# Moving the second half's normalisation behind the first ropes, and the second ropes' sums to Pool, in the prologue of an attention and routed-MLP kernel

## The reference

```
xn  = layernorm(x)
q, k = rope(xn @ Wq.T), rope(xn @ Wk.T); v = xn @ Wv.T      # 16 heads of 16
attn = softmax(mask(q k^T / 4)) v @ Wo.T
xm  = three-tap mix of xn along the tokens
ffn = layernorm(xn + (the one of 9 two-layer paths that the router picks for the token), gamma, beta)
out = x + attn + ffn
```

## Time and profile before

| | us |
|---|---|
| three runs | 888.17, 888.21, 890.82 |
| median | 888.21 |
| profiled execution, device time | 890.88 |
| span of the profiled execution | 889.1 |
| PE busy | 808.8 (91%) |
| VectorE busy | 627.8 (71%) |
| ScalarE busy | 478.3 (54%) |
| Pool busy | 289.7 (33%) |
| mean granted clock of PE (1.0 is full speed) | 0.964 |

### The profile page before, as it was taken

The page is one execution under the profiler, slowest core; times in us unless marked ns, Lnnn a source line. Parts: engine busy times, 40 slices in busy tenths (PEclk is TensorE's granted clock), DMA queues, the critical chain, the costliest instruction groups (busy, mean ns, idle before and its releaser), DMA issues.

```text
span 889.1 us, 13041 instructions
## 1 busy us (share of the span) xinstructions
PE 808.8 (91%) x4968; PEld 396.1 (45%) x4968; DVE 627.8 (71%) x1222; ACT 478.3 (54%) x820; POOL 289.7 (33%) x420
## 2 busy tenths in 40 slices
PE   4767999989999999989999999989999999999986
PEld 2422334344455534344355544435355554354434
DVE  5967786757678697658759688666868777767521
ACT  2452545645545655655646655655646555555572
POOL 1001023860515121781513302495140502030523
PEclk9876999989999999989999999999999999999999
DMA  6372312124222413022350623021450330300103
GB/s 214 107 177 45 75 28 45 36 72 107 51 46 46 97 49 72 1 72 76 67 96 1 119 72 64 10 72 37 108 95 2 72 73 17 56 1 1 25 1 72
DMA packets 35386, 55.15 MB, mean 62 GB/s; under 512 B 4330, under 2 KB 31667, under 8 KB 32444
## 3 DMA queue, kind: packets, MB, share of 16 engines
q1 hardware_dynamic: 30812, 49.54, 24.0%
q0 software_dynamic: 4224, 4.19, 3.2%
q10 hardware_dynamic: 288, 0.59, 0.2%
HBM read 37.27 MB, written 16.78 MB: 61 GB/s over the span
## 4 chain that ended last, share of the span: by engine, by line
PE 72%; DVE 15%; POOL 8%; ACT 2%; issue 2%; DMA 1%; SPq 1%; DVEq 0%; ACTq 0%; POOLq 0%
PE bank L1210 13%; PE bank L1171 12%; PE bank L1191 12%; PE bank L1157 8%; PE bank L1147 6%; DVE piecemax L991 5%; PE bank L1238 3%; PE bank L1168 3%; PE bank L1102 3%; PE bank L1113 2%; PE bank L1220 2%; PE bank L1120 2%; POOL prob L653 2%; POOL turned L635 2%; POOL raw L636 2%
## 5 line engine op out<-in xcount | busy, mean ns | idle before, releaser
L991 DVE TENSOR_REDUCE piecemax<-bank 128x1 f32<-128x512 f32 (+3 forms) x608 | 381.8, 656 | 181.4 <-PE bank L1171 179.6
L774 ACT ACTIVATE prob<-bank 128x512 f32<-128x512 f32 x576 | 334.4, 597 | 315.7 <-PE bank L1191 313.9
L653 POOL TENSOR_SCALAR_AFFINE_SELECT prob<-prob 128x256 f32<-128x256 f32 (+1 forms) x320 | 134.0, 433 | 429.2 <-ACT prob L774 428.0
L1171 PE MATMUL bank<-k_st,q_st 96*128 96x128 bf16 (+3 forms) x1152 | 231.4, 281 | 11.6 <-DVE piecemax L991 11.4
L1191 PE MATMUL bank<-q_st,k_st 98*128 98x512 bf16 (+3 forms) x768 | 223.3, 332 | 12.5 <-DMA q_st<-shiftT 6.4
L1210 PE MATMUL bank<-prob,v_sb 128*17 128x512 f32 (+3 forms) x1536 | 159.8, 505 | 13.3 <-POOL prob L653 13.1
L1171 PEld LDWEIGHTS bank<-k_st,q_st 96*128 96x128 bf16 x1152 | 98.6, 99 | 146.9 <-issue 63.6
L1191 PEld LDWEIGHTS bank<-q_st,k_st 98*128 98x128 bf16 x768 | 71.5, 99 | 120.7 <-ACT prob L774 51.5
L1157 PE MATMUL bank<-w_sb,mid 128*128 128x256 f32 (+1 forms) x320 | 86.7, 394 | 3.2 <-DVE z L984 3.2
L1102 PE MATMUL bank<-xnT,wqk_sb 128*128 128x512 f32 x128 | 68.3, 635 | 5.6 <-ACT xnT L709 4.7
L1147 PE MATMUL bank<-xm,w_sb 128*128 128x512 f32 x128 | 67.6, 609 | 0.0
(11 more groups left out here) (86 smaller groups left out, 721.3 us busy)
## 6 DMA issues: line engine op xcount, KB each, us to landing
scratch<-parts SPq DMA_DIRECT2D x16, 768.0 KB, 3.8
q_st<-scratch SPq DMA_DIRECT2D x90, 128.0 KB, 6.8
k_st<-scratch SPq DMA_DIRECT2D x15, 384.0 KB, 4.7
z<-in_x SPq DMA_DIRECT2D x8, 512.0 KB, 4.8
z<-in_x POOLq DMA_DIRECT2D x8, 512.0 KB, 6.0
out<-z SPq DMA_DIRECT2D x8, 512.0 KB, 3.3
k_st<-scratch SPq DMA_DIRECT2D x15, 256.0 KB, 5.4
k_st<-scratch SPq DMA_DIRECT2D x17, 128.0 KB, 5.7
```

Source lines behind the costliest of these rows:

```text
L653: nc.gpsimd.affine_select(out=d, in_=d, compare_op=ALU.is_ge, fill=0.0, base=0, pattern=pattern, channel_multiplier=-1).then_inc(masked, 1)
L774: nc.scalar.activation(prob[:, place_of(G, i), :], ps[:, :], ACT.Exp, scale=float(DK) ** -0.5).then_inc(act_took, 1)
L991: nc.vector.tensor_reduce(piecemax[:, G % 2, t, h:h + len(cols), piece], ps[:, 0:len(cols) * w].rearrange("p (h k) -> p h k", k=w), AX.X, ...
L1171: ins = nc.tensor.matmul(ps[:, k * w:(k + 1) * w], q_st[0:PARTS, G % STACKS, h, t * P:(t + 1) * P], k_st[0:PARTS, G % STACKS, h, k0:k0 + w ...
```

## The change

Two things change, both for batch 0 only.

1. In the prologue's list stats, pow and norm of the second half no longer stand ahead of the first projections. They stand behind the first half's four projections, two ropes and two hi cuts, and directly ahead of the transposes of the second half.
2. The two sums of the second half's ropes (q and k) are formed by Pool (L637, L638) and no longer by VectorE (L906, L907). VectorE still forms the products out of PSUM. Pool waits for VectorE's second unit of the rope. The predicate `sums_on_dve(n, half)` takes the place of `rope_on_dve(n)` where the semaphore and its count are chosen.

```diff
-    head("load", 0, 0)
-    head("load", 0, 1)
-    for half in range(2):
+    def normalized(half):
         head("stats", 0, 0, half)
         head("pow", 0, 0, half)
         head("norm", 0, half)
-        if half == 0:
-            turn(0)
+
+    head("load", 0, 0)
+    head("load", 0, 1)
+    normalized(0)
+    turn(0)
     project(0, 0)
     cut(0, 0, "hi")
     project(1, 0)
     cut(1, 0, "hi")
+    normalized(1)
     turn(1)
     cut(0, 0, "rest", "mid_cut")
     cut(1, 0, "rest", "mid_cut")
...
+def sums_on_dve(n, half):
+    return n == 0 and half == 0
...
-    mine = [x for x in ORDER if x[0] == "rope" and rope_on_dve(x[1]) == rope_on_dve(n)]
+    mine = [x for x in ORDER if x[0] == "rope" and sums_on_dve(x[1], x[3]) == sums_on_dve(n, half)]
...
-            return (roped_dve if rope_on_dve(n) else roped_pool), nth_rope(n, qk, half)
+            return (roped_dve if sums_on_dve(n, half) else roped_pool), nth_rope(n, qk, half)
...
-                pool.wait_ge(tables_loaded, 32)
-                pool.wait_ge(act_took, TOOK["qk", n, qk, 1, half])
-                if k >= 2:
-                    pool.wait_ge(lo_cut, NTH["lo", *from_turn(k - 2)])
-                nc.gpsimd.tensor_tensor(a, r, half_of(cos_sb, half)[:, None, :].to_broadcast(shape), ALU.mult)
-                link(nc.gpsimd.tensor_tensor(r, r, half_of(sin_sb, half)[:, None, :].to_broadcast(shape), ALU.mult))
+                if rope_on_dve(n):
+                    pool.wait_ge(dve_took, TOOK["qk", n, qk, 1, half])
+                else:
+                    pool.wait_ge(tables_loaded, 32)
+                    pool.wait_ge(act_took, TOOK["qk", n, qk, 1, half])
+                    if k >= 2:
+                        pool.wait_ge(lo_cut, NTH["lo", *from_turn(k - 2)])
+                    nc.gpsimd.tensor_tensor(a, r, half_of(cos_sb, half)[:, None, :].to_broadcast(shape), ALU.mult)
+                    link(nc.gpsimd.tensor_tensor(r, r, half_of(sin_sb, half)[:, None, :].to_broadcast(shape),
+                                                 ALU.mult))
                 nc.gpsimd.tensor_tensor(a[:, 0, :], a[:, 0, :], r[:, 1, :], ALU.subtract)
                 nc.gpsimd.tensor_tensor(a[:, 1, :], a[:, 1, :], r[:, 0, :], ALU.add).then_inc(roped_pool, 1)
...
                 elif what == "rope":
-                    if not rope_on_dve(name[1]):
+                    if not sums_on_dve(name[1], name[3]):
                         rope(*name[1:])
...
-                elif what == "rope" and rope_on_dve(name[1]):
+                elif what == "rope" and sums_on_dve(name[1], name[3]):
                     rope(*name[1:])
```

## The result

| | before | changed |
|---|---|---|
| first comparison, median of 5 | 890.74 us (888.17 to 891.87) | 896.80 us (895.27 to 900.03) |
| ratio, 95% interval | | 1.0078 (1.0048 to 1.0107) |
| second comparison, ratio | | 1.0094 (1.0081 to 1.0107) |
| span of the profiled execution | 889.1 us | 898.0 us |

The change makes the kernel slower by a little under 1%: by 7 us in the first comparison and by 8 in a second one on another set of runs. The ratios are of the means of the runs, so they need not agree with the quotient of the medians (6.1 us apart here). 7.0 was forecast, 895.2 us and a range of 892.0 to 899.3; the median 896.80 lies in it.

What follows compares the result with a forecast made beforehand. The prologue's VectorE chain was taken to set when the body begins. With the last cut at 52.0 against 45.04, 7.0 us pass on whole: median 888.21 becomes 895.2 us, range 892.0 to 899.3.

Steps and rivals of the forecast that it cites:

- What bounds: Prologue: VectorE's chain to the last cut sets when the body begins; a microsecond there is one on the end.
- Rivals 3: Body: a different phase of engines or clock gives back 4 to 7 us; 888 to 890.8; chance 0.06.
- 4 (the clock turns it round): PE's clock in 56 to 60 and 72 to 88: up to 7.6 us back, 885.0, faster; chance 0.03.
- rival 2: Maxima or next stretch: PE's longer rests leave its clock low, 2.65 us on top, up to 899.3; chance 0.11.
- First ropes: First half on VectorE: units taken at 16.76 and 18.46, sums done at 24.7 instead of 25.69, 1.0 us earlier.
- Normalisation in the open: Second half after the first ropes: 5.23 us uncovered, plus 0.6 for Pool's cast beside the root; done at 30.6.
- Transposes: Second half on PE from 30.8: 1.94 us instead of 1.03, as PE stands still for 9 us beforehand.
- Second projections: PE from 33.6 instead of 27.39, at the first half's pace; last product 43.6; high end 1.35 us later.
- Sums on Pool: Second ropes: 2.5 us a pair, saving VectorE only about 1.2 of 2.4; last cut 52.0, 7.0 us later.
- The meeting: L913 on VectorE and Pool's sum in the second rope shut each other out; 1.15 us on the last cut.
- The covers: First-half stacks there by 51.2 at the latest, before VectorE is free at 52.0; V projections hidden under the cuts.
- Last cut and first score matmul: End of prologue: last cut about 52.0 instead of 45.04, first score matmul near 63.8 instead of 56.77.

Runs made afterwards that it cites:

- the delay run: The kernel before with ten linked additions (0.7 us each, results unused) on VectorE ahead of the last four cuts; ratio 1.0068 (1.0051 to 1.0086), 6.0 us.
- the run with a busy PE: The changed kernel with eight extra unused matmuls on PE between the first projections and the second half's transposes; ratio 1.0063 (1.0047 to 1.0078).
- part 2 alone: The kernel before with only the sums of the second half's ropes moved to Pool, the normalisation where it stood; ratio 1.0008 (0.9997 to 1.0019).
- the fourteen traces: One execution each: kernel before and changed kernel twice, ten follow-up variants once; first score matmul from 55.30 to 65.02, body 828.8 to 833.0 us.

## Why the prediction was right

- **What bounds.** "So the prologue sets when the body begins", and the delay is "passed on whole". Shown by the delay run: 5.4 to 5.8 us at the first score matmul, 6.0 in time. Rivals 3 (given back in the body) and 4 (the clock turns it round) fall, and so does rival 2's loss in the next stage as far as the spans can show it: the body covers the same range in both kernels.
- **First ropes.** Units were forecast to be taken at 16.76 and 18.46 and the ropes done at 24.7, 1.0 us ahead of before. In the two traces they were taken at 17.26 and 19.62, and at 17.42 and 19.07; the ropes were done at 25.88 and 25.3. The first copy was 0.15 and 0.5 us late in these executions, the rest is PE's records, which stayed 0.86 us apart for longer (16 of them in 9.61 and 8.73 us, against 8.56). So in the first trace nothing was left of that 1.0 us. This is the term of the chain that was off by most, by 1.2 and 0.6 us: the working took the pace of the records from one trace.
- **Normalisation in the open.** 5.23 + 0.6 us forecast, 5.67 measured (25.88 to 31.55). The 0.6 for the cast was 0.36, shown by taking it away.
- **Transposes.** 1.94 forecast, 1.97 measured. That it is the clock is shown by the run with a busy PE (1.10).
- **Second projections.** The last product was forecast to be written at 43.6, 10.0 us after the projections' start at 33.6; it was at 45.1 and 44.1 in the two traces, 10.7 and 10.2 us after theirs (34.45 and 33.91). Most of the lateness is thus inherited from the first ropes. The alternative that was kept as the high end (+1.35) did not happen; the choice of the first half's course was off by 0.7 and 0.2.
- **Sums on Pool.** The step as forecast: pairs of 2.5 us, a subtraction that stands until Pool's sum ends, a last sum of 2.25 (2.4 forecast). The meeting cost 0.97 us, not 1.15. The Trainium skill (SBUF — State Buffer, "SBUF: two separate sides") calls this an exclusive lock on a shared port pair, and the runs agree: both meetings went away with the overlap. The text said that the move saves "only about 1.2" of 2.4 us on VectorE and left the net open; by the first score matmul of part 2 alone it is a loss of about 1.9, of which the times confirm 1.7 at most. From the last product to the last cut it took 8.2 us in both traces, 8.4 forecast.
- **The covers.** PE began the maxima of the changed kernel at 50.52 (51.2 forecast) and VectorE was free for them at 53.25, so the first half's stacks stayed off the path.
- **Last cut and first score matmul.** Forecast 52.0 and 63.8; 53.34 and 65.02, 52.34 and 64.78. Against the mean of before the first score matmul moved by 7.9, not 7.0, and the last cut by 8.3. Beside the first ropes it is the base that was off: the last cut of before was taken from one trace, 45.04 (43.95 in the other), and the distance from it to the first score matmul, 11.7 us, as fixed. It is 11.7 to 13.3 in the fourteen traces. That the two traces of the changed kernel had on average the shorter landings (5.2 us against 5.6) took 0.4 us off the shift, which is luck. That the ratio of the first comparison, 1.0078, falls on 7.0 us to the tenth is luck too; the second one gave 8.4.

## What to carry to other kernels

Work that sits under another engine's matmuls costs nothing; moved to where the other engine waits for it, it costs its full length, and then the other engine's lower clock on top. Giving two dependent sums to a slower engine helps only where something else fills the time until they are needed: here it moved the first score matmul back by 1.9 us at the end of the chain, and won 1.2 at the last cut where it stood ahead of k's rope. And before shortening a chain, look at what stands beside its end, and at more than one trace: 3.0 us off the last cut brought 1.5 against one trace of the kernel before and 1.9 off it brought 1.9 against the other, because the landing of the stores differed.

## What the runs showed of the hardware

- PE's 16 projection records of the first half took from 8.54 to 10.06 us in executions with the same work ahead of them. So the wait for a projected unit differs by over a microsecond from one execution to the next, in kernels that do the same.
- The body differs by over 4 us from one execution to the next of one kernel. In the fourteen traces it falls into two groups some 3 us apart. The runs without a trace do not: 26 of the 57 spans of the kernel before lie from 887.0 to 888.3 us, with 57.0 for the prologue a body of 830.0 to 831.3, between the two groups. Compared from the first score matmul by the starts of Pool's pow instructions, all fourteen lie within 1.6 us of one another some 269 us on, and the difference grows later, not in the same stretch in each. What makes it was not found.
- A pair of stores of 768 KB moves 340 GB/s and lands 4.9 us after its last cut in seven traces. In seven others, in which a packet of 16 KB of the instruction queue ran beside it, it lands after 5.6 to 6.5 us, with a tail in which one of the 16 DMA engines is busy. A queue's issue order doesn't show this; the DMA share by stretch does.
